# A sorted mixture-of-experts kernel: block outputs written whole and gathered back, and sixteen early blocks at the head of the block table

## The reference

```python
x = x + recurrence(layernorm(x))          # gated complex linear scan over the 512 tokens
h = layernorm(x)                          # 2048 tokens
scores = sigmoid(h @ gate_w.T)            # 32 experts in 8 groups; the best 4 groups, then the best 6 experts
w, idx = top6(scores in the best groups); w = 2.5 * w / sum(w)
y = sum over the 6 experts e of w_e * (silu(h @ w11[e].T) * (h @ w33[e].T)) @ w22[e].T
x = x + y + shared_expert(h)              # silu(h @ sw1.T) * (h @ sw3.T) @ sw2.T
```

## Time and profile before

| | |
|---|---|
| median of 3 runs | 449.61 us (448.42 to 450.6) |
| profiled execution | 450.83 us, of which the span from the first to the last instruction is 449.1 us |
| PE, DVE, ACT, POOL busy | 84%, 66%, 58%, 52% of the span |
| DMA | 87.70 MB, mean 195 GB/s |
| first transposes of the block loop | 228.40 us |
| last block output (L992) | starts 431.70 us |

### The profile page before, as it was taken

The page is one execution under the profiler, slowest core; times in us unless marked ns, Lnnn a source line. Parts: engine busy times, 40 slices in busy tenths (PEclk is TensorE's granted clock), DMA queues, the critical chain, the costliest instruction groups (busy, mean ns, idle before and its releaser), DMA issues.

```text
span 449.1 us, 9145 instructions
## 1 busy us (share of the span) xinstructions
PE 376.1 (84%) x2120; PEld 301.2 (67%) x2121; DVE 294.3 (66%) x990; ACT 260.7 (58%) x585; POOL 231.6 (52%) x242
## 2 busy tenths in 40 slices
PE   2777696965976778399889999999999998998935
PEld 2644263745645563155579999999999997997924
DVE  3669688999988824612235555555567777777982
ACT  2678978768575132011157777767777776776710
POOL 2000000752778777777516666666656665663750
PEclk9898867595785687689999999999999999999996
DMA  8990000220335999333347666666689889879724
GB/s 241 405 339 2 0 0 1 74 102 15 118 118 201 413 430 380 130 128 128 117 145 215 188 195 182 204 188 191 191 265 354 255 248 300 303 208 336 244 83 174
DMA packets 41850, 87.70 MB, mean 195 GB/s; under 512 B 7204, under 2 KB 32295, under 8 KB 41296
## 3 DMA queue, kind: packets, MB, share of 16 engines
q1 hardware_dynamic: 28384, 54.77, 36.7%
q0 software_dynamic: 10704, 30.07, 18.6%
q10 hardware_dynamic: 2720, 2.40, 1.7%
HBM read 49.81 MB, written 39.71 MB: 199 GB/s over the span
## 4 chain that ended last, share of the span: by engine, by line
PE 50%; DVE 19%; ACT 9%; DMA 8%; issue 8%; POOL 3%; DVEq 1%; SPq 1%; ACTq 0%; POOLq 0%
PE PS L1228 17%; PE PS L1235 8%; PE PS L1165 7%; DMA payload_and_xn_t<-choice_rows 5%; PE PS L1220 4%; PE PS L1121 3%; POOL choice_rows L441 3%; PE PS L1178 3%; DMA resid<-in_x 2%; PE PS L1076 2%; ACT L605 1%; DVE st L682 1%; PE PS L1261 1%; ACT payload_and_xn_t L555 1%; DMA choice_rows<-block_out_s,block_meta 1%
## 5 line engine op out<-in xcount | busy, mean ns | idle before, releaser
L441 POOL DMA_INDIRECT choice_rows<-block_out_s,block_meta x127 | 127.0, 1000 | 86.0 <-issue 58.3
L427 POOL DMA_INDIRECT bucket_rows<-payload_and_xn_t,dest x96 | 101.9, 1062 | 116.2 <-DVE dest L874 88.2
L1228 PE MATMUL PS<-block_rows_t,block_gate_up_weights 128*128 128x128 f32 x1016 | 134.9, 276 | 0.0
L1228 PEld LDWEIGHTS PS<-block_rows_t,block_gate_up_weights 128*128 128x128 f32 x1016 | 123.4, 192 | 1.1 <-ACT block_rows_t L630 0.9
L625 ACT ACTIVATE block_gate_up_weights<-expert_weights 128x512 f32 x127 | 80.0, 630 | 35.6 <-issue 29.6
L1235 PE MATMUL PS<-expert_weights,block_hidden_t 128*128 x254 | 76.3, 382 | 3.8 <-DVE block_hidden_t L985 3.8
L992 DVE TENSOR_SCALAR block_out_s<-PS,block_meta 128x256 f32<-128x256 f32 x127 | 61.2, 482 | 0.0
L985 DVE TENSOR_TENSOR block_hidden_t<-block_silu_t,PS 128x128 f32<-128x128 f32 x127 | 36.3, 286 | 24.2 <-ACT block_silu_t L617 22.0
L630 ACT ACTIVATE block_rows_t<-PS 128x256 f32<-128x256 f32 x127 | 46.5, 366 | 7.6 <-PE PS L1220 7.6
L1220 PE MATMUL PS<-ident,block_rows_s 128*128 128x128 f32 x254 | 48.6, 273 | 1.4 <-DVE resid L964 1.3
L980 DVE COPY block_meta<-block_rows_s 128x2 f32 x127 | 22.0, 173 | 41.7 <-issue 41.4
(11 more groups left out here) (185 smaller groups left out, 459.1 us busy)
## 6 DMA issues: line engine op xcount, KB each, us to landing
block_rows_s<-bucket_rows SPq DMA_DIRECT2D x127, 160.0 KB
payload_and_xn_t<-choice_rows SPq DMA_DIRECT2D x16, 768.0 KB, 6.5
bucket_rows<-pad_rows SPq DMA_DIRECT2D x1, 5120.0 KB, 26.3
expert_weights<-in_experts SPq DMA_DIRECT2D x1, 4224.0 KB, 14.0
expert_weights<-in_experts SPq DMA_DIRECT2D x1, 3456.0 KB, 16.3
expert_weights<-in_experts SPq DMA_DIRECT2D x1, 2688.0 KB, 18.3
resid<-in_x SPq DMA_DIRECT2D x4, 512.0 KB, 9.3
choice_rows<-block_out_s,block_meta POOLq DMA_INDIRECT x127, 3.2
```

What stands on the lines that cost most here:

```text
L427: nc.gpsimd.indirect_dma_start(out=bucket_ap[:, :], out_offset=bass.IndirectOffsetOnAxis(ap=dest[:, t, k:k + 1], axis=0), in_=PAY[:, t, :] ...
L441: nc.gpsimd.indirect_dma_start(out=choice_ap[0:rows, :], out_offset=bass.IndirectOffsetOnAxis(ap=meta_id[:, slot, 1:2], axis=0), in_=yy[:, ...
L1228: ins = mm(PS[:, 2 + r, g * P:(g + 1) * P], ws[:, r, (2 * k + g) * P:(2 * k + g + 1) * P], xT[:, r, k * P:(k + 1) * P], start=(k == 0), st ...
```

## The change

Three things change together.

1. **Whole blocks out, rows gathered back.** SP writes each block's output as one contiguous 128 x 256 piece to `bucket_outputs`, 11 blocks behind the loads. POOL no longer scatters in the loop; it gathers, for each tile and each choice, 128 rows from there (96 gathers) into a ring of 4 tiles (6 before). DVE works out where each row will be (`output_rows`, `output_sources`). The rows in the buckets lose the interleaved numbers (288 instead of 320 elements). DVE adds one choice in every step from step 59 on, 48 of them in a loop of two turns (`ADD_TURNS`) with addresses from a register, and 26 of the 96 behind the last step. PE's sum of tile 14 is gone. All stores are issued by SP.
2. **Early blocks.** `early_blocks`, 22 operations on DVE ahead of `choose(4)`, finds sixteen whole blocks that hold rows of the first eight tiles only. They lead the table; SP waits only for chunks 0 to 2 before it loads them, and for the others behind them.
3. **Order and phases.** Nine phases (ends at tiles 2, 4, 6, 8, 10, 12, 14, 15, 16) instead of five. PE does `positions(4)` and `(5)` ahead of `shared_gate_up(0, 1)`, and `(1, 0)` ahead of the table's products, which are four. `shared_hidden` of batch 0 moves around the table's operations. In the prologue SP fills `bucket_outputs` with zeros in five transfers. The loops are unrolled by 8 instead of 16.

```diff
-    ROW = D + 2 * E
+    ROW = D + E
-    LP = 16
+    LP = 8
-    PHASE_ENDS = (1, 2, 3, 4, 5)
+    CUTS = [[2], [2], [2, 4], [2, 4], [2], [1, 2]]
-    RING = 6
+    RING = 4
+    TURN_ADDS = RING * TOPK
+    EARLY_BLOCKS = 16
+    EARLY_TILES = 8
+    FIRST_ADD = 59
+    WRITE_LAG = NXS + 3
...
         def blocks_through(phase):
-            b, t0, nt = CHUNKS[PHASE_ENDS[phase]]
-            bound = ((b * TS + t0 + nt) * P * TOPK + E * (P - 1)) // P
-            return -(-bound // NXS) * NXS if phase == 0 else bound
+            return max((PHASE_TILES[phase] * P * TOPK + E * (P - 1)) // P, EARLY_BLOCKS + E)
...
+            for n in range(NCH - 1):
+                part = slice(n * BLOCKS // (NCH - 1), (n + 1) * BLOCKS // (NCH - 1))
+                sp.wait_ge(s_gp, n + 1)
+                sp.dma_start(outputs_ap[part.start * P:part.stop * P].rearrange("(j p) d -> p j d", p=P),
+                             PADT[:, 0:D].unsqueeze(1).to_broadcast([P, part.stop - part.start, D])).then_inc(s_clear, 16)
...
-            for i in range(NCH):
-                sp.wait_ge(s_scat[i], 16 * TOPK * CHUNKS[i][2])
+            rows_scattered(0, early_chunks)
...
+            def load_block(j, u, taken):
+                if u % 4 == 0:
+                    sp.reg_load(first_rows, tabs[0:1, bass.ds(j, 4)])
                 if taken is not None:
                     sp.wait_ge(s_xtp, taken)
                     sp.wait_ge(s_meta, taken)
-                row = sp.value_load(tabs[0:1, bass.ds(j, 1)], min_val=0, max_val=E * CAP - P)
+                row = sp.snap(first_rows[u % 4], min_val=0, max_val=PLANE - P)
+            def write_block(j, u):
+                if u % 4 == 0:
+                    sp.reg_load(first_outputs, tabs[0:1, bass.ds(j + 3 * P, 4)])
+                sp.wait_ge(s_y, j + 1)
+                row = sp.snap(first_outputs[u % 4], min_val=0, max_val=2 * P * P - P)
+                sp.dma_start(outputs_ap[bass.ds(row, P), :], yy[:, u % NY, :]).then_inc(s_ys[u % NY], 16)
...
+            for j in range(EARLY_BLOCKS):
+                load_block(j, j, j - NXS + 1 if j >= NXS else None)
+                if j >= WRITE_LAG:
+                    write_block(j - WRITE_LAG, j - WRITE_LAG)
+            rows_scattered(early_chunks, NCH)
+            with sp.Fori(EARLY_BLOCKS, FIRST_STORE, LP) as i:
+                for u in range(LP):
+                    load_block(i + u, u, i + (u - NXS + 1))
+                    write_block(i + (u - WRITE_LAG), (u - WRITE_LAG) % LP)
...
-            def scatter(j, slot, ready, rows):
...
+            def gather_outputs(n):
+                all_written(pool, blocks_through(phase_of(n)))
+                pool.wait_ge(s_src, n // TS + 1)
+                if n < RING:
+                    pool.wait_ge(s_resid, B)
+                for k in range(TOPK):
+                    if n >= RING:
+                        pool.wait_ge(s_added, added(n - RING, k))
+                    nc.gpsimd.indirect_dma_start(
+                        out=RINGS[:, n % RING, k, :], out_offset=None, in_=outputs_ap[0:BLOCKS * P, :],
+                        in_offset=bass.IndirectOffsetOnAxis(ap=source[:, n, k:k + 1], axis=0)).then_inc(s_cin[n % RING][k], 16)
...
-                c.add(V.tensor_tensor_scan(rank[:, n, :].rearrange("p t e -> p (t e)"), flat_memb, flat_memb, 0.0, AD, ALU.bypass))
-                c.add(STT(PAY_id[:, rows, D + 1::2], rank[:, n, :], float((NT - 1 - tile) * P * TOPK),
-                          idb[:, n].unsqueeze(2).to_broadcast([P, nt, E]), AD, AD))
...
+            for s in range(LP + 3):
+                step(s, s)
+            with dve.Fori(LP + 3, FIRST_ADD, LP) as i:
+                for u in range(LP):
+                    step(i + u, u + 3)
+            with dve.Fori(0, ADD_TURNS, 1) as turn:
+                for u in range(TURN_ADDS):
+                    step(turn * TURN_ADDS + (FIRST_ADD + u), FIRST_ADD + u)
+                    add_choice(*divmod(u, TOPK), turn)
...
             shared_gate_up(0, 0)
+            positions(4)
+            positions(5)
             pe.wait_ge(s_xn2, NCH)
             shared_gate_up(0, 1)
-            positions(4)
-            positions(5)
+            shared_gate_up(1, 0)
             pe.wait_ge(s_dest, NCH)
             pe.wait_ge(s_tabf, 3)
```

More of the change, by code:

```diff
@@ L962, in shared_out, with output_sources @@
+            def output_sources(g):
+                at_least(dve, s_src, g)
+                dve.wait_ge(s_added, 1)
+                for t in range(TS):
+                    c.add(V.max(dv[:, t, :], dpos[:, g * TS + t, :]))
+                c.wait()
+                TSC(source[:, g * TS:(g + 1) * TS, :], dv[:, :, 0:TOPK], -1.0, None, AD).then_inc(s_src, 1)
             def shared_out(b):
@@ L1023, in _, with add_choice @@
-            for s in range(LP):
+                    take_meta(s, u % NMETA, loads)
+            def add_choice(n, k, turn=None):
+                slot = n % RING
+                if turn is None:
+                    dve.wait_ge(s_cin[slot][k], 16 * (n // RING + 1))
+                    dve.wait_ge(s_added, added(n, k) - 1)
+                    total = resid[:, n, :]
+                else:
+                    dve.wait_ge(s_cin[slot][k], turn * 16 + 16)
+                    dve.wait_ge(s_added, turn * TURN_ADDS + (added(n, k) - 1))
+                    total = resid_row[:, bass.ds(turn * (RING * D) + n * D, D)]
+                TT(total, total, RINGS[:, slot, k, :], AD).then_inc(s_added, 1)
@@ L1024, in _ @@
+            for s in range(LP + 3):
                 step(s, s)
-            with dve.Fori(LP, UNROLL_AT, LP) as i:
+            with dve.Fori(LP + 3, FIRST_ADD, LP) as i:
                 for u in range(LP):
-                    step(i + u, u)
-            for s in range(UNROLL_AT, BLOCKS + 2):
-                step(s, s)
-                for n in range(NT):
-                    if n in ADD_AT and ADD_AT[n] <= s < ADD_AT[n] + TOPK // ADD_RATE[n]:
-                        for _ in range(ADD_RATE[n]):
-                            add_choice(*divmod(adds["done"], TOPK))
@@ L1040, in _ @@
+            for m in range(done, NT * TOPK):
+                add_choice(*divmod(m, TOPK))
         @block.tensor
```

433 lines of the change are left out of this document (240 added, 193 removed).

## The result

The changed kernel took 462.22 us in the median (460.40 to 462.33, 4 runs), the kernel before 450.11 (448.42 to 450.67, 4 runs). The ratio is 1.0266 with an interval of 1.0227 to 1.0305: slower by 2.7%, 2.2 us above the top of the predicted range. The profiled execution took 462.33 us around a span of 460.5.

The account below looks back on a forecast made before the run. POOL's queue of 24 gathers bounds the end: block 114's write landed at 415.0, last gather at 444.6, landing, addition and store to 449.6, plus 1.0 for SP's lag: span 450.6, median 451.1 us. Range 445.5 to 460.

Parts of the forecast that it names:

- a queue on POOL behind the write of block 114: Tail: 24 gathers queued on POOL set the end, by itself 448.0 to 454.0 us; chance 0.55.
- the cost of DVE's loop: Block loop, steps 59 to 128: one addition a step on DVE taken as 0, bounds 0 and 0.42 us.
- the loop starts at 227.4: Head: the block loop's start at 227.4 us instead of 228.4, 1.0 us earlier; bounds 224.4 and 229.9.
- The slow start: Head: PE's first products after idling behind the table run slowly, costing 2.8 us.
- 0.7 for stalls: Block loop: 0.7 us left for new small waits, counted ahead of block 114's write landing.
- Landing 2.3: Tail: the write of block 114 lands 2.3 us after it, at 415.0 us.
- 23 x 1.28 = 29.4: Tail: the last of 24 gathers on POOL starts 29.4 us after the first, at 1.28 us each.
- 1.0 for SP's lag: Tail: 1.0 us added to 449.6 for SP running late, giving a span of 450.6.
- the additions hold up some of the gathers: Rival, tail: DVE's additions delay POOL's gathers by 0.42 us in each of 24, 10 us, 461; chance 0.03.
- The head: Rival, head: no slow start and cheaper early blocks, loop starts at 223, span 446.8, faster; chance 0.14.
- The last block sets the end: Rival, tail: the last block's own path, not the queue, ends the kernel at 443, faster; chance 0.07.
- DVE by its looped additions: Rival, loop: register work of looped additions binds DVE, 48 steps x 0.3 = 14 us, 465, slower; chance 0.07.

Follow-up runs that it names:

- c1_unroll_cut_lag: The changed kernel with DVE's additions written out, a phase cut at tile 13 and blocks written 9 loads behind; span 447.5 us, median level with the kernel before.
- f3_gates_no_drain: The changed kernel with additions written out, writes 9 loads behind, a phase for each of tiles 8 to 16, no final POOL drain; 443.84 us, ratio 0.9859.
- b4: The changed kernel with POOL waiting for the last addition before its program ends; span 461.7 us.

## Why the prediction was wrong

The likeliest case, a queue on POOL behind the write of block 114, took place, and the gathers in it cost what was said. Two steps of the prediction failed: the cost of DVE's loop (5.1 us), and the end of the program behind the last store, where POOL's drain had no term (4.6 us). A third term, the landing of the write, was too small by 2.6 us. The forecast of 450.6 us for the span missed by 9.9 in all, and these are the terms, from the working in the order in which it was made:

- **Head, "the loop starts at 227.4": 226.0, -1.4.** The column was ready at 189.0, where the steps give 190.5 - 1.8 = 188.7. The slow start was 1.8 instead of 2.8, and the shared product could begin at 190.1 instead of 190.6. The 22 early operations took 4.8 us, from 162.72 to 167.52, where 5 was said. (The table operations from 180.39 to 185.3 that this price comes from are 17, not 16.)
- **"0.7 for stalls", and "117 x 1.546" up to the write of block 114: +5.1.** It was issued 190.35 us after the first transposes instead of 185.3. The step that failed is the cost of the loop on DVE: it priced the looped addition by its register work, which does cost next to nothing, and left out the jump back over a body of 24 written-out steps. That jump cost 5.8 us of loop (shown by writing it out), some 3.5 of it the stall and 2.3 the lower clock behind it. With the loop written out the write is issued 184.5 us after the first transposes, so without the jump this term would have been 0.8 us too long.
- **"Landing 2.3": 4.9, +2.6.** The 2.28 us came from the one last scatter of the kernel before. Its trace had the spread of all 127 (line L441), and 2.28 is as short as the shortest of them:

```profile
DMA to landing us min/median/max: 2.3/3.2/7.0
```

  The last scatter lands where the transfer engines are nearly idle, and the write of block 114 lies amid loads, writes and gathers. That this load is the reason fits the spread and these two windows, before and after (next to last number: the share of the transfer engines that is busy), but no run tried it:

```profile
428.00:437.00 9.00, 2.64 (x15) 1.62 (x14) 8.56 (x24) 0.75 (x4) 5.31 (x5) 0.93 0.12 30
```

```profile
416.00:422.00 6.00, 6.00 (x49) 5.60 (x48) 4.82 (x18) 4.59 (x13) 1.69 (x2) 1.00 0.84 265
```

- **"23 x 1.28 = 29.4, with 0.15 for the first wait": 29.21, -0.3.** A gather takes 0.95 with 0.30 before it, 1.25; the other 0.46 us are a few longer ones.
- **From the last gather to the last addition, 2.95: 3.24, +0.3.**
- **"Store 2.1" and "1.0 for SP's lag": +3.7.** SP had no lag, and the store and end took 2.2 where nothing else held them (-0.9). POOL's drain, for which there was no term, added 4.6 (shown by taking it out). It stood in the trace of before too, hidden under loads and stores.

With the -1.4 of the head this makes 10.0, the 9.9 and rounding. The three large late terms (5.1, 2.6 and 3.7) all concern what starts the queue or comes behind it, none the queue itself.

Of the steps that cost nothing: the early lead gave nothing (shown). SP's two transfers a step fit (its waits, and no wait of PE for block rows). DVE's loop with an addition in each step kept 1.546 us a step where it doesn't jump. The zeros weren't tried by themselves; the head that they lie in came no later than forecast. Nor was the head's 2.4 us split among the shorter rows, the new order and the wider table.

One rival did take place, at a small fraction of its price: the additions hold up some of the gathers. Timeline of the changed kernel:

```profile
351.05 0.43 DVE L1133 TENSOR_TENSOR resid<-resid,payload_and_xn_t 128x256 f32 x1
351.15 1.14 POOL L478 DMA_INDIRECT payload_and_xn_t<-bucket_outputs,output_rows  x1 [0.30 <-issue]
...
352.60 0.95 POOL L478 DMA_INDIRECT payload_and_xn_t<-bucket_outputs,output_rows  x1 [0.30 <-issue]
352.92 0.43 DVE L1133 TENSOR_TENSOR resid<-resid,payload_and_xn_t 128x256 f32 x1 [0.32 <-issue]
```

From 305 to 430 us, 5 of 79 gathers begin 0.06 to 0.12 us after an addition has begun. They take 1.12 to 1.18 us, and none of the other 74 over 0.98. In `c1_unroll_cut_lag`, from 300 to 422 us, it is 16 of 86, up to 1.21 us, and none of the others over 0.99. So a gather that begins within some 0.2 us behind an addition's start is held, by up to 0.26 us, and one that begins ahead of it is not. In the last row this is three gathers and 0.4 us, not the 10 us of the rival. The contention that the prediction set aside for these transfers is thus there; the one scatter that it looked at didn't show it. No run took the additions out to measure the sum.

The other rivals did not take place. The head gave 2.4 us, not 5.4. The last block sets the end only when the queue is mended (`f3_gates_no_drain`). SP and DVE by its looped additions didn't bind. The slow side did come out, by two mechanisms that no rival had: a stall at a jump back, and work that POOL leaves for its drain. The range ended at 460.0.

## What to carry to other kernels

Ask what a loop's jump back costs on each engine, by the length of its body. Here nothing was to be seen for 8 steps on DVE, and 3.7 us for 24, with PE's clock on top, at the one jump of that kind. Take the landing time of a transfer from the spread of many in the trace, and from a stretch with the DMA load of the place where it will stand, not from one in an idle tail. And read who holds the last instruction of the program: POOL, which issues the 96 gathers, needed 8.9 us to drain behind the last one, and 4.6 of them were added to the span. A second drain in an earlier pause gave 4.1 us back in the median; leaving the drain out gave 3.9, in a program that waits for every transfer elsewhere.

## What the hardware showed beyond that

POOL's drain behind its indirect transfers, from the end of the last one to its own end: 2.0 us after 223 scatters, 2.7 after these and one gather, 7.9 after 96 scatters with 48 or 72 gathers, 8.6 with 92, 8.9 with 96 (8.9 or 9.0 in each of twelve profiled executions, of which one, `b4`, counts from the drain's own start); 3.9 for 48 gathers that came after an earlier drain. It runs as long when it begins after all has landed. What it works off isn't settled: it falls neither in step with the gathers nor with semaphores. The two figures for 48 gathers, 7.9 behind 96 scatters and 3.9 without them, hint that the scatters have a part in it, in a kernel with gathers; no run left the scatters out or drained right behind them.
